# Hard graph attention with residual and layer norm: three steps of the item loop in another order on ScalarE and VectorE

## Chip, cores and metric

One core of a Trainium2 chip. The metric is the device time in microseconds (us) of the whole program, median of several runs.

## What is computed

```python
Q, K, V = (x @ W.T).reshape(n, 8, 32).transpose(1, 0, 2)      # n = 4096, one W each
attn = einsum('hqd,hkd->hqk', Q, K) * 32 ** -0.5 + (Q @ we.T + be)
attn = attn + where(adj > 0, 0.0, -inf)
attn = softmax(attn, axis=-1)
hard = (attn == max(attn, axis=-1, keepdims=True)) / 8
out  = einsum('hqk,hkd->hqd', hard, V).transpose(1, 0, 2).reshape(n, 256)
y    = layernorm(x + out)                                     # over 256 columns
```

Only the best permitted key of each query and head counts. The adjacency matrix is thin, and thinner for later rows.

## The kernel before

**Tiling.** 4096 rows are 32 tiles of 128 rows, a tile is 4 groups of 32 queries. The keys that at least one query of a group reaches are listed, and an item is up to 372 of them (3 chunks of 124). The loop scores 201 items here. For each item the kernel finds the key numbers, gathers rows of keys and values from `kv_table` in HBM, scores them, finds the minimum of the negated scores for each row and half of the heads, marks the winners, and adds their values to `o_all`.

**The loop.** After a first part (projections, table, the lists of 4 tiles) every engine runs the same loop. A turn is four bodies, b = 0 to 3, one item further each. Flags, planned by SyncE and read from memory, say whether a turn also has: the *front end* of a tile (`fe_on`: adjacency cast to bf16 in four quarters, packed into words), its *finish* (`fin_on`: ranks and lists), and *rows due* (`te_on`: transpose, residual and layer norm of a finished tile). A turn with none of them is called plain here. Engines meet only through semaphores, and each takes its instructions in the order written.

**Body b on each engine, in order** (item numbers relative to the turn):

- TensorE: `planes_of(b+4)` (L1207), `scores(b+1)` (L1222, L1227), `words` of a cast quarter (L1162) if there is one, `values(b-1)` (L1257), `hards_across(b)` (L1237), `keys_across(b+2)` (L1245), and for b = 1 `rows_back` (L1267). `words` and `values` wait for the merge of the item before.
- ScalarE: `masks(b+2)` (L656), `hard_rows(b)` (L652, waits for `hards_across(b)`), `owners(b+5)` (L624: the owner matrix `reached`, which `planes_of` of that item needs), `keys(b+2)` (L662, both halves), then the extras (b = 1: cast 1; b = 2: cast 3 at L605 and behind it `row_std` at L673), `hards(b+1)` (L667, waits for the minimum), and for b = 0 and 1 casts 0 and 2.
- VectorE: `pick(b+4)` (L928, L934, L941, L943: key numbers and mask bits), the extras, `tops(b+1)` (L951 `best`, L955 `minus_top`, L958 `keep`), for b = 2 `norm_rows` (L992 `rstd`, L995 `y_out`, which waits for ScalarE's `std`), and `merge(b-1)` (L968, two instructions).
- GpSimd: a copy of the queries (L525) and `gather(b+3)` (L532: three indirect DMAs, one for a chunk), which waits for the picks of its item.

`owners(b+5)` waits for `planes_of(b+3)` (two buffers `reached`), a step that TensorE does before `scores(b)`.

Of the kernel before, what the change touches and what calls it, by code (L numbers as in the profile page):

```python
# [5 lines left out]
ALU = mybir.AluOpType  # L6
# [32 lines left out]
def hard_attention(nc, x, adj, wq, wk, wv, we, be, out):  # L39
# [24 lines left out]
    with ExitStack() as ctx:  # L64
# [192 lines left out]
        def for_loop(eng, r, k):  # L257
            def value(s, j=0):
                ahead = k + j - lag[s.name]
                return r["n"] if ahead == 0 else eng.snap(r["n"]) + ahead  # L260
            return value
# [80 lines left out]
        def tile_of(eng, r, k):  # L342
            return eng.snap(r[k]) & (2 * T - 1)
# [239 lines left out]
        def _(act):  # L583
# [70 lines left out]
            def masks(m, due):  # L654
                act.wait_ge(dve_bits, due(dve_bits))
                act.activation(masked[m % RING][0:USED], bits[m % RING][0:USED].rearrange("p c l k -> p c (l k)")  # L656
                               .unsqueeze(2).to_broadcast([USED, CHUNKS, HEADS4, GQ]), ACT.Relu, bias=one[0:USED],
                               scale=-1.0).then_inc(act_masked, 1)
# [23 lines left out]
            def turn():  # L682
                def cast_quarter(i):
                    with front_end(act, r):
                        cast(tile_of(act, r, "fe") * 16 + 16, tile_of(act, r, "fe") * QUARTERS, i)

                for b in range(RING):
                    masks(b + 2, for_loop(act, r, 2))
                    hard_rows(b, for_loop(act, r, 0))
                    owners(b + 5, for_loop(act, r, 5), f"ahead{b + 5}")  # L690
                    for h in range(HALVES):
                        keys(b + 2, for_loop(act, r, 2), h)
                    if b == 0:
                        with front_end_finish(act, r):
                            flags_back(tile_of(act, r, "fin") + 1)
                    if b == 1:
                        cast_quarter(1)
                    if b == 2:
                        cast_quarter(3)
                        with rows_due(act, r):  # L700
                            row_std(tile_of(act, r, "te_done"))
                    if b == 3:
                        take_plan()
                    hards(b + 1, for_loop(act, r, 1))
                    if b == 0:
                        cast_quarter(0)
                    if b == 1:
                        cast_quarter(2)
                    act.reg_add(r["n"], r["n"], 1)
# [13 lines left out]
        def _(dve):  # L723
# [224 lines left out]
            def tops(m, due, at, between=None):  # L948
                dve.wait_ge(pe_score[0], due(pe_score[0]))
                dve.wait_ge(pe_score[1], due(pe_score[1]))  # L950
                dve.tensor_reduce(best[:], ps_both[m % 2][:, :, 0:SLOTS], AX.X, ALU.min).then_inc(dve_best, 1)  # L951
                if between is not None:
                    between()
                capped = cap_of[:].rearrange("p g i -> p (g i)")[:, bass.ds(at, 1)]
                dve.scalar_tensor_tensor(out=minus_top[m % 2][:], in0=minus_top[(m + 1) % 2][:], scalar=capped,  # L955
                                         in1=best[:], op0=ALU.max, op1=ALU.min
                                         )._wait_ge(dve_best, due(dve_best)).then_inc(dve_minus, 1)
                dve.scalar_tensor_tensor(out=keep[m % RING][:], in0=minus_top[(m + 1) % 2][:], scalar=capped,  # L958
                                         in1=minus_top[m % 2][:], op0=ALU.max, op1=ALU.is_equal
                                         )._wait_ge(dve_minus, due(dve_minus)).then_inc(dve_keep, 1)  # L960

            def merge(m, due, group):
                width = PARTS * HD
# [98 lines left out]
            def turn(begun=True):  # L1062
                def fin():
                    return tile_of(dve, r, "fin")

                def table():
                    return (dve.snap(r["fin"]) & (TABLES - 1)) * GPT

                for b in range(RING):
                    if b == 2:  # L1070
                        with front_end_finish(dve, r):
                            rank_steps(fin() + 1, fin() * FIN, table(), for_loop(dve, r, 4)(pe_planes))
                    pick(b + 4, for_loop(dve, r, 4), next_flags if b == 3 else None, "ahead8" if b == 0 else f"ahead{b + 4}")
                    if b == 1:
                        with front_end_finish(dve, r):
                            ranks(fin() + 1, fin() * FIN, None)
                            lists(fin() * FIN, table(), fin() * GPT)
                        with rows_due(dve, r):
                            odd = bits_of(dve, r["te_done"], 1)
                            with dve.If_lt(odd, 1):  # L1080
                                turn_rows(0, for_loop(dve, r, -2)(dve_merge))
                            with dve.If_ne(odd, 0):
                                turn_rows(GPT, for_loop(dve, r, -2)(dve_merge))
                    if b == 2:
                        with rows_due(dve, r):
                            norm_stats(tile_of(dve, r, "te_done"))
                    tops(b + 1, for_loop(dve, r, 1), listed(f"listed{b + 1}"),
                         (first_places, lambda: step_plan(dve, r), ended_places, next_places)[b])
                    if b == 0:
                        with front_end_finish(dve, r):  # L1090
                            dve.wait_ge(pe_pv, for_loop(dve, r, -1)(pe_pv))
                            word_steps(fin() + 1, fin() * FIN, table())
                    if b == 3:
                        with front_end(dve, r):
                            dve.wait_ge(pe_pv, for_loop(dve, r, -1)(pe_pv))
                            words(tile_of(dve, r, "fe") * QUARTERS, tile_of(dve, r, "fe") * FIN)
                        dve.reg_add(r["fe"], r["fe"], r["fe_on"])
                        dve.reg_mov(r["fe_on"], r["fe_next"])
                    if b == 2:
                        with rows_due(dve, r):  # L1100
                            norm_rows(tile_of(dve, r, "te_done"))
                    if b > 0 or begun:
                        merge(b - 1, for_loop(dve, r, -1),
                              dve.snap(r[f"running{b - 1}" if b else "running_last"], min_val=0, max_val=(2 * GPT - 1) * HALVES * PARTS * HD))
                    dve.reg_add(r["n"], r["n"], 1)

            turn(False)
# [294 lines left out]
```

## Time and profile before

| | us |
|---|---|
| median of 3 runs | 1316.35 |
| lowest, highest | 1309.31, 1316.83 |
| the profiled execution, its own time | 1317.37 |
| its span, first to last instruction | 1315.6 |
| busy in the span: TensorE matmul, VectorE, ScalarE, GpSimd | 951.6, 929.0, 892.0, 632.8 |
| VectorE `best` L951, 201 instructions | 190.7 |
| first and last `best` start at | 180.9, 1279.8 |

The mean granted TensorE clock of the span is 0.918 of full speed. No engine is busy over 72% of the span. The item loop lies between 181 and 1280 us, so about 1099 us for 200 bodies.

### The profile page before, as it was taken

The page shows a single profiled execution, that of the slowest core. Times are in us where ns is not written, and L with a number is a line of the kernel's source. Part 1 is how long each engine was busy: PE and PEld are TensorE (multiplying, and loading weights), DVE is VectorE, ACT ScalarE, POOL GpSimd, SP SyncE. Part 2 cuts the span into 40 slices and gives each one's busy share as a digit, 9 for nine tenths or more (in the row PEclk, how much of TensorE's full clock was granted, in tenths as well). Part 3 has the DMA queues.
Part 4 walks back from the last instruction along what each step waited for, and adds up shares of the span by engine and source line. Part 5 has one row for each costly group of instructions (what it writes and reads, how often), then busy time and mean ns, then how long its engine had stood idle before and what let it go on. Part 6 is the DMA issues. An engine that isn't in the chain of part 4 may idle for free.

```text
span 1315.6 us, 51593 instructions
## 1 busy us (share of the span) xinstructions
PE 951.6 (72%) x14758; PEld 616.6 (47%) x14759; DVE 929.0 (71%) x2616; ACT 892.0 (68%) x1688; POOL 632.8 (48%) x820
## 2 busy tenths in 40 slices
PE   4787648777777778777787777777777777777771
PEld 2343325454544555455454545455445545455540
DVE  5444536777878777777787777777777777778880
ACT  1523347778777787777877877877777777766770
POOL 0000065675656566555565555554554455445650
PEclk9988877999999998989999899989998989989995
DMA  4634468677687787678777878778878787756770
GB/s 155 214 128 160 145 201 279 196 231 255 197 263 217 243 253 234 215 242 266 248 207 231 268 226 262 252 230 272 257 235 258 248 251 254 254 180 194 212 213 4
DMA packets 89522, 291.06 MB, mean 221 GB/s; under 512 B 16984, under 2 KB 30040, under 8 KB 89496
## 3 DMA queue, kind: packets, MB, share of 16 engines
q0 software_dynamic: 48720, 199.60, 49.5%
q1 hardware_dynamic: 40776, 91.15, 20.4%
q8 instruction: 12, 0.20, 0.1%
q14 instruction: 14, 0.11, 0.0%
HBM read 275.98 MB, written 14.71 MB: 221 GB/s over the span
## 4 chain that ended last, share of the span: by engine, by line
DVE 26%; PE 25%; issue 20%; ACT 15%; DVEq 7%; DMA 3%; ACTq 2%; SPq 1%; POOL 1%; POOLq 0%
DVE best L951 6%; ACT joined L605 5%; PE ps_both L1222 4%; ACT k_t L662 4%; PE ps_both L1154 4%; DVE picks L941 3%; PE ps_h L1237 3%; PE ps_o L1257 3%; DVE hit_vals L934 3%; PE ps_r L1267 3%; DVE hit L928 2%; PE ps_both L1227 2%; ACT hard L667 2%; PE ps_both L1144 2%; DVE o_all L968 2%
## 5 line engine op out<-in xcount | busy, mean ns | idle before, releaser
L532 POOL DMA_INDIRECT kv<-kv_table,picks x309 | 294.9, 954 | 231.3 <-DVE picks L941 127.6
L532 POOL DMA_INDIRECT early<-kv_table,picks x300 | 286.2, 954 | 246.0 <-DVE picks L941 131.6
L652 ACT ACTIVATE hard_t<-ps_h 128x768 bf16<-128x768 bf16 x200 | 162.0, 810 | 233.1 <-PE ps_h L1237 227.4
L667 ACT ACTIVATE hard<-ps_both,minus_top 128x384 bf16<-128x384 f32 x402 | 214.1, 594 | 32.9 <-DVE minus_top L955 30.3
L1222 PE MATMUL ps_both<-k_t,q_now 32*32 32x384 f32 x3216 | 192.6, 534 | 32.1 <-ACT k_t L662 29.0
L951 DVE TENSOR_REDUCE best<-ps_both 128x2 f32<-128x768 f32 x201 | 190.7, 949 | 28.0 <-PE ps_both L1227 17.8
L1207 PE MATMUL ps_x<-pay,reached 128*128 x1224 | 120.2, 233 | 99.6 <-ACT reached L624 93.3
L662 ACT COPY k_t<-ps_both 128x384 f32<-128x384 f32 x404 | 171.6, 479 | 14.4 <-PE ps_both L1245 14.3
L968 DVE SCALAR_TENSOR_TENSOR o_all<-o_all,keep,ps_o 128x96 f32 x400 | 107.7, 311 | 61.8 <-issue 26.5
L1207 PEld LDWEIGHTS ps_x<-pay,reached 128*128 128x128 bf16 x1224 | 83.7, 102 | 137.5 <-ACT reached L624 128.0
L605 ACT ACTIVATE joined<-adj_in,minus_half 128x1024 bf16<-128x1024 int32 x128 | 147.9, 1164 | 0.0
L1227 PEld LDWEIGHTS ps_both<-mask_of,masked 128*128 128x128 bf16 x1206 | 72.9, 102 | 140.9 <-issue 140.9
L525 POOL COPY q_now<-q_t 128x64 f32 x202 | 50.4, 249 | 167.4 <-issue 164.3
L656 ACT ACTIVATE masked<-bits,one 124x384 bf16<-124x384 uint32 x202 | 127.6, 631 | 1.4 <-issue 1.4
L624 ACT ACTIVATE reached<-iota_h,edge_of 128x384 bf16<-128x384 f16 x205 | 124.1, 605 | 1.3 <-DVE pay L906 0.8
L1227 PE MATMUL ps_both<-mask_of,masked 128*128 128x128 bf16 x1206 | 109.4, 231 | 0.0
L1237 PE MATMUL ps_h<-ident_b,hard 128*128 128x128 bf16 x1200 | 107.6, 229 | 0.0
L941 DVE TENSOR_REDUCE picks<-hit_vals 128x9 uint32<-128x288 f32 x204 | 92.7, 455 | 15.1 <-DVE hit_vals L934 9.8
L934 DVE TENSOR_TENSOR hit_vals<-ps_x,hit 128x288 f32<-128x288 f32 x204 | 93.3, 458 | 7.0
L1245 PE MATMUL ps_both<-ident_f,kv 128*128 128x128 f32 x612 | 87.6, 281 | 12.0 <-DMA kv<-kv_table,picks 12.0
L1245 PE MATMUL ps_both<-ident_f,early 128*128 128x128 f32 x600 | 90.5, 291 | 1.6 <-DMA early<-kv_table,picks 1.6
L928 DVE SCALAR_TENSOR_TENSOR hit<-ps_x,slot_of,slot 128x96 f32<-128x96 f32 x204 | 64.0, 314 | 31.5 <-issue 16.1
(145 smaller groups left out, 1309.5 us busy)
## 6 DMA issues: line engine op xcount, KB each, us to landing
adj_in<-in_adj SPq DMA_DIRECT2D x128, 512.0 KB, 5.7
kv_table<-early SPq DMA_DIRECT2D x32, 320.0 KB, 2.4
kv<-kv_table,picks POOLq DMA_INDIRECT x309
early<-kv_table,picks POOLq DMA_INDIRECT x300
early<-in_x SPq DMA_DIRECT2D x8, 512.0 KB, 6.8
x_row<-in_x SPq DMA_DIRECT2D x32, 128.0 KB
out<-y_out SPq DMA_DIRECT2D x32, 128.0 KB
plan<-places_of SPq DMA_DIRECT2D x212, 0.0 KB
```

Of the source, the lines that this page charges most:

```text
L532: pool.indirect_dma_start(kv[m % KVS][:, c, :], None, kv_table, bass.IndirectOffsetOnAxis(ap=picks[m % RING][:, c, 2:3], axis=0)).then_inc ...
L605: act.activation(joined[:, i * QW:(i + 1) * QW], adj_in[:, i * QW:(i + 1) * QW], ACT.Sign, bias=minus_half[:]).then_inc(act_cast, 1)
L652: act.activation(hard_t[m % 2][:], hard_rows_t, ACT.Copy, bias=1.0).then_inc(act_hard_t, 1)
L662: act.copy(k_t[m % 2][:, h, :], ps_s[m % 2][h][:, 0:SLOTS]).then_inc(act_kt[h], 1)
L667: done = act.activation(hard[m % 2][:, h, :], ps_s[m % 2][h][:, 0:SLOTS], ACT.Sign, bias=minus_top[m % 2][:, h:h + 1], scale=-1.0)
L951: dve.tensor_reduce(best[:], ps_both[m % 2][:, :, 0:SLOTS], AX.X, ALU.min).then_inc(dve_best, 1)
L968: done = dve.scalar_tensor_tensor(out=o_run, in0=o_run, scalar=keep[m % RING][:, h:h + 1], in1=ps_o[:, h * width:(h + 1) * width], op0=ALU ...
L1207: mm = pe.matmul(ps_x[:, c * P:(c + 1) * P], reached[m % 2][:, c * P:(c + 1) * P], pay[:].rearrange("p g i v -> p (g i v)") [:, bass.ds(va ...
L1222: pe.matmul(ps_s[m % 2][h][to:to + GQ, 0:SLOTS], q_now[m % RING][head:head + HD, h, :], k_t[m % 2][head:head + HD, h, :], start=True, stop ...
L1227: mm = pe.matmul(bank[:, c * P:(c + 1) * P], masked[m % RING][:, c, :, :].rearrange("p h q -> p (h q)"), mask_of[:], start=False, stop=(c ...
L1237: mm = pe.transpose(hard_rows_t[:, at:at + P], hard[m % 2][:, h, c * P:(c + 1) * P], ident_b[:])
L1245: mm = pe.transpose(ps_s[m % 2][h][:, c * P:(c + 1) * P], kv[m % KVS][:, c, h * P:(h + 1) * P], ident_f[:])
```

## The change

On ScalarE `owners(b+5)` goes to the head of the body, ahead of `masks` and `hard_rows`; in body 2 `row_std` goes ahead of cast 3. On VectorE `keep` is computed from `best` itself (is_le in place of is_equal against `minus_top`), ahead of `minus_top`, which then carries no wait of its own; in body 2 `merge` goes ahead of `norm_rows`. No instruction is added or taken out, and nothing else changes.

```diff
                 for b in range(RING):
+                    owners(b + 5, for_loop(act, r, 5), f"ahead{b + 5}")
                     masks(b + 2, for_loop(act, r, 2))
                     hard_rows(b, for_loop(act, r, 0))
-                    owners(b + 5, for_loop(act, r, 5), f"ahead{b + 5}")
...
                     if b == 2:
-                        cast_quarter(3)
                         with rows_due(act, r):
                             row_std(tile_of(act, r, "te_done"))
+                        cast_quarter(3)
...
+                dve.scalar_tensor_tensor(out=keep[m % RING][:], in0=minus_top[(m + 1) % 2][:], scalar=capped,
+                                         in1=best[:], op0=ALU.max, op1=ALU.is_le
+                                         )._wait_ge(dve_best, due(dve_best)).then_inc(dve_keep, 1)
                 dve.scalar_tensor_tensor(out=minus_top[m % 2][:], in0=minus_top[(m + 1) % 2][:], scalar=capped,
-                                         in1=best[:], op0=ALU.max, op1=ALU.min
-                                         )._wait_ge(dve_best, due(dve_best)).then_inc(dve_minus, 1)
-                dve.scalar_tensor_tensor(out=keep[m % RING][:], in0=minus_top[(m + 1) % 2][:], scalar=capped,
-                                         in1=minus_top[m % 2][:], op0=ALU.max, op1=ALU.is_equal
-                                         )._wait_ge(dve_minus, due(dve_minus)).then_inc(dve_keep, 1)
+                                         in1=best[:], op0=ALU.max, op1=ALU.min).then_inc(dve_minus, 1)
...
+                    if b > 0 or begun:
+                        merge(b - 1, for_loop(dve, r, -1), ...)
                     if b == 2:
                         with rows_due(dve, r):
                             norm_rows(tile_of(dve, r, "te_done"))
-                    if b > 0 or begun:
-                        merge(b - 1, for_loop(dve, r, -1), ...)
```

## Rows read from the trace of the kernel before

**Rows 1.** The page, part 4: the chain that ended last, by engine.

```profile
DVE 26%; PE 25%; issue 20%; ACT 15%; DVEq 7%; DMA 3%; ACTq 2%; SPq 1%; POOL 1%; POOLq 0%
```

**Rows 2.** Timeline, one plain body: start us, us, engine, line, what, [idle before].

```profile
286.54 0.81 ACT L652 ACTIVATE hard_t<-ps_h 128x768 bf16<-128x768 bf16 x1 [0.86 <-PE ps_h L1237]
...
287.25 0.60 ACT L624 ACTIVATE reached<-iota_h,edge_of 128x384 bf16<-128x384 f16 x1
...
287.75 0.85 ACT L662 COPY k_t<-ps_both 128x384 f32<-128x384 f32 x2
...
287.90 0.56 PE L1207 MATMUL ps_x<-pay,reached 128*128 x6 [0.74 <-ACT reached L624]
...
288.74 0.88 PE L1222 MATMUL ps_both<-k_t,q_now 32*32 32x384 f32 x16 [0.28 <-ACT k_t L662]
...
290.91 0.81 ACT L652 ACTIVATE hard_t<-ps_h 128x768 bf16<-128x768 bf16 x1 [0.86 <-PE ps_h L1237]
```

**Rows 3.** Line 951 (`best`) in 299 to 878 us and 878 to 1203 us: how many bodies.

```profile
L951 DVE TENSOR_REDUCE best<-ps_both x109: 919/951/959, 298.9 to 878.0; 128x2 f32<-128x768 f32 x109
...
L951 DVE TENSOR_REDUCE best<-ps_both x53: 918/951/958, 878.0 to 1202.7; 128x2 f32<-128x768 f32 x53
```

**Rows 4.** Waits of VectorE, 299 to 878 us: total us, times, longest.

```profile
DVE rstd L992 <- ACT std L673: 35.9, 14, 3.2
```

**Rows 5.** Waits of VectorE, 878 to 1203 us.

```profile
DVE pay L906 <- PE ps_x L1207: 13.0, 13, 2.0
...
DVE rstd L992 <- ACT std L673: 6.7, 11, 0.8
```

**Rows 6.** Timeline, body 2 of a turn with front end and rows due.

```profile
606.25 0.18 DVE L988 BATCH_NORM_AGGREGATE mean_var<-stats 128x2 f32<-128x6 f32 x1
...
607.55 0.81 ACT L652 ACTIVATE hard_t<-ps_h 128x768 bf16<-128x768 bf16 x1 [0.92 <-PE ps_h L1237]
...
609.49 1.17 ACT L605 ACTIVATE joined<-adj_in,minus_half 128x1024 bf16<-128x1024 int32 x1
...
610.54 0.30 ACT L673 ACTIVATE std<-mean_var,eps 128x1 f32<-128x1 f32 x1
...
610.95 0.16 DVE L992 RECIPROCAL rstd<-std 128x1 f32<-128x1 f32 x1 [3.06 <-ACT std L673]
...
611.58 0.54 DVE L968 SCALAR_TENSOR_TENSOR o_all<-o_all,keep,ps_o 128x96 f32 x2
```

**Rows 7.** The chain in order of time, `minus_top` to merge: start us, us.

```profile
627.10 0.27 DVE minus_top L955
627.40 0.08 DVE keep L958
...
627.74 0.08 DVE o_all L968
```

**Rows 8.** Timeline of VectorE, three instructions with no wait between them.

```profile
581.41 0.29 DVE L881 SCALAR_TENSOR_TENSOR rank<-ps_x,flag 128x128 f32<-128x128 f32 x1 [0.26 <-issue]
581.62 0.15 DVE L883 COPY ends<-ps_x 128x4 f32<-128x4 f32 x1
581.68 0.15 DVE L884 SCALAR_TENSOR_TENSOR count_f<-ps_x,flag 128x4 f32<-128x4 f32 x1
```

**Rows 9.** Timeline of GpSimd in a plain turn: the first gather of three bodies running.

```profile
351.87 0.97 POOL L532 DMA_INDIRECT early<-kv_table,picks  x1 [0.16 <-issue]
...
357.39 0.97 POOL L532 DMA_INDIRECT early<-kv_table,picks  x1 [0.81 <-issue]
...
361.27 0.97 POOL L532 DMA_INDIRECT early<-kv_table,picks  x1 [0.16 <-issue]
```

**Rows 10.** Waits of ScalarE over the span.

```profile
ACT hard L667 <- DVE minus_top L955: 30.3, 38, 2.8
```

**Rows 11.** Timeline near the loop's start: scores at half clock, and VectorE behind planes.

```profile
198.97 1.53 PE L1222 MATMUL ps_both<-k_t,q_now 32*32 32x384 f32 x16
199.00 0.32 DVE L928 SCALAR_TENSOR_TENSOR hit<-ps_x,slot_of,slot 128x96 f32<-128x96 f32 x1 [1.80 <-PE ps_x L1207]
```

More of the change, by code:

```diff
@@ L1098, in turn @@
                         dve.reg_mov(r["fe_on"], r["fe_next"])
+                    if b > 0 or begun:
+                        merge(b - 1, for_loop(dve, r, -1),
+                              dve.snap(r[f"running{b - 1}" if b else "running_last"], min_val=0, max_val=(2 * GPT - 1) * HALVES * PARTS * HD))
                     if b == 2:
@@ L1101, in turn @@
                             norm_rows(tile_of(dve, r, "te_done"))
-                    if b > 0 or begun:
-                        merge(b - 1, for_loop(dve, r, -1),
-                              dve.snap(r[f"running{b - 1}" if b else "running_last"], min_val=0, max_val=(2 * GPT - 1) * HALVES * PARTS * HD))
                     dve.reg_add(r["n"], r["n"], 1)
```

## Prediction

> **What bounds the kernel now.** I read the page's chain first [rows 1]: no engine holds it; VectorE and TensorE have a quarter each, ScalarE 15%, and a fifth is issue, time in which an engine works through its own registers and waits. So two circles compete, and I looked for each in the timeline.
>
> The first is TensorE and ScalarE. In a plain body [rows 2] ScalarE starts `hard_rows` at 286.54, `owners` at 287.25, `keys` at 287.75; TensorE's planes wait for `owners`, its scores for `keys`; `values` and `hards_across` follow, and the next `hard_rows` starts at 290.91, the moment these end. One round is 4.37 us, and ScalarE has idled 0.86 us in front of `hard_rows`.
>
> The second is VectorE. From 299 to 878 us there are 108 bodies in 579.1 us, 5.36 each [rows 3]. Its one long wait there is `rstd` behind ScalarE's `std`: 35.9 us in 14 turns [rows 4]. Without it a body would be 5.03, nearly solid work and issue. From 878 to 1203 us every turn has everything in it: 52 bodies, 6.24 each, with only 6.7 us behind `std`, and 13.0 us in 13 waits for planes in front of L906 [rows 5]. VectorE is the bound there.
>
> Rows 6 show the stall whole. `mean_var` is ready from 606.43. ScalarE does `hard_rows` at 607.55, then owners and keys, then cast 3 at 609.49, and only then `std` at 610.54. VectorE has idled 3.06 us when `rstd` starts at 610.95, and its merge, which TensorE's next words and values wait for, comes at 611.58.
>
> **The change part by part.**
>
> *Owners first.* `owners` lies between `hard_rows` and `keys` and takes 0.50 us of that circle (287.25 to 287.75) [rows 2]. In front, it lies in the 0.86 us in which ScalarE waits for `hards_across`, so it costs nothing there; with that cover gone it would cost the same 0.50 again, so it never loses. Its own wait, planes of two items before, is over by then: TensorE does these ahead of the scores whose minimum the `hards` just before it in ScalarE's queue waited for. The circle falls from 4.37 to 3.87 in a plain body. Planes are no longer late either, as `reached` is there first. The gain counts only where this circle is the bound.
>
> *`std` ahead of cast 3, merge ahead of `norm_rows`.* `hard_rows` to cast 3 is 1.94 us, of which owners is 0.50; so `std` would start at 607.55 + 1.44 = 608.99 in place of 610.54, and `rstd` could start 0.41 later, at 609.40 [rows 6]. VectorE meanwhile does its merge (0.54 and its issue) first and is ready for `rstd` at about 608.6. In the phase of rows 6, 0.8 of the 3.06 us would be left. But the circle has by then run two bodies with 0.50 less each, so I take it that only the register work of about 0.2 us is left. Behind `std` in ScalarE's queue are cast 3 and `hards(3)`; `hards(3)` waits for a later VectorE result than `mean_var` in any case, and cast 3 comes 0.3 us later than it could. The merge comes at about 608 in place of 611.58, so TensorE no longer waits for it. Cost of the two moves on VectorE: nothing, the same instructions.
>
> Gain: 35.9 - 14 x 0.2 = 33.1 us in 299 to 878, and 6.7 - 11 x 0.2 = 4.5 us in 878 to 1203 [rows 4, 5].
>
> *`keep` first.* Now `minus_top` starts at 627.10, `keep` at 627.40, merge at 627.74 [rows 7]: 0.64 us, with `keep` and merge each behind a semaphore of the instruction just ahead. After it `keep` starts where `minus_top` did, `minus_top` needs no wait, and merge's wait is over while `minus_top` runs. Three instructions with no wait between them start 0.21 and 0.06 apart though they take 0.29 and 0.15: each starts some 0.08 ahead of the last one's end [rows 8]. So `minus_top` starts about 0.14 to 0.25 after `keep`, and merge 0.38 to 0.52 after it in place of 0.64. The trace shows no such pair of 128x2 instructions, so the bounds are 0.26 (merge issue alone decides) and 0.12 (strict order, the wait gone), and 0 if merge's issue work cannot start earlier. I take 0.18, in between, since the nearest rows overlap.
>
> The Trainium skill (VectorE: DVE Perf Modes, The DRAIN you can't avoid) says that chaining ops without semaphores saves nothing, as the next op waits for the pipe to empty; by that rule the sum would have nothing for `keep`. Rows 8 speak against it here, with starts ahead of the previous end; the page's own later section on two instructions with no wait allows an earlier start.
>
> The price: `minus_top` ends 0.14 to 0.26 us later after `best`, and `hards`, the cast behind it, and `hards_across` with it. ScalarE waits for `minus_top` in 38 of 200 bodies today [rows 10]. Where VectorE is the bound this comes back as nothing, since `hards` has a body's time until `hards_across`.
>
> *Where VectorE's gain stops.* In a plain turn GpSimd's gathers start 5.52 apart once and 3.88 apart otherwise [rows 9]: 5.52 + 3 x 3.88 = 17.2 us for four bodies, 4.29 a body, whatever the others do. Plain turns (20 bodies, 12 of them before 299 us) can thus hardly go under that; without this floor both circles would allow about 3.9. In 878 to 1203 body 1 of each turn waits for planes behind `rows_back` [rows 5], so what VectorE saves in that body is lost: 13 bodies.
>
> **The sum.**
>
> - 181 to 299 us, 24 bodies: in the first 8 the first circle binds (VectorE waits 1.80 for planes [rows 11]): 8 x 0.50 = 4.0. 4 more at 0.18: 0.7. 12 plain at 4.37 - 4.29: 1.0. Together 5.7.
> - 299 to 878: 33.1 for `std`; `keep` in 100 of 108 bodies (8 are plain): 18.0. I take off 3 for gathers that come late behind the two plain turns, and 3 for bodies in which the later `minus_top` does hold ScalarE. Together 45.
> - Can the first circle follow? It takes at most 5.36 a body now and loses 0.50: 4.86 or less. VectorE would be at 5.03 - 0.18 = 4.85. It can, just.
> - 878 to 1203: 4.5 for `std`, 39 bodies x 0.18 = 7.0: 11.5.
> - 1203 to 1280, 16 bodies x 0.18: 2.9.
>
> In all 65 us. The profiled execution took 1317.37, 1.0 above the median of the runs, so the sum gives 1252 by it and 1251 by the median: I say **1252**.
>
> **The rivals.**
>
> *The order of `keep` gives nothing* (strict order, or merge's issue work decides). For it: register work lies between `keep` and merge. Against it: rows 8. It takes away 0.7 + 18.0 + 7.0 + 2.9 = 28.6 us: 1281.
>
> *The first circle becomes the bound.* Casts stand behind `hards`, `hards` waits for a later `minus_top`, and words, values and `hards_across` stand behind the casts. If the 0.50 of owners counts in only half of the 108 bodies, that stage gives 27 in place of 45, and the rest about 15: 42 us, 1275. For it: 4.86 against 4.85 is no margin. Against it: much of the 5.36 is TensorE's wait for the late merge, which goes.
>
> *The stall stays.* `std` waits for `mean_var`, now with cast 3 queued behind it, and `keep` gives nothing: only the first 8 bodies gain, about 1310, no change. Against it: `mean_var` was ready 1.1 us before `hard_rows` began [rows 6].
>
> *Slower: the TensorE clock.* At the lower level (1.2 of 2.4 GHz) scores take 1.53 us in place of 0.88 [rows 11, 2]; scaled to planes, hards and keys too I estimate 2 us more a body. Planes now come right behind `keys_across` and leave one longer gap ahead of scores. If that gap lowers the clock in many bodies, it eats the gain: it takes about 32 more slow bodies to reach no gain and 40 to be 1% slower. TensorE is as busy for each item as before in less time, which speaks against it: 1335.
>
> **How the numbers follow.** Forecast 60% (its own range 1238 to 1268: `keep` at 0.12 to 0.26 moves it by 10 us either way, the two allowances by 6), `keep` for nothing 16%, first circle 12%, stall stays 6%, clock 6%. The range 1235 to 1283 takes in the first three but for their tails. 1% is 13 us, about what a measurement of this kernel tells from no change: faster 0.89, same 0.06, slower 0.05.
>
> **What would show it.** Right: the wait of `rstd` falls from 43 us in all to under 10; `owners` fills the idle time ahead of `hard_rows`; in a plain body `hard_rows` to `keys` is 0.71; `keep` to `minus_top` starts 0.14 to 0.25 apart and merge under 0.45 after `keep`; VectorE's waits for planes and best stay small; in plain turns GpSimd has no wait. Wrong: `rstd` still waits over 1 us; `best` waits for scores in most bodies (first circle); `minus_top` to merge is unchanged; a mean clock well under 0.918.

## The result, and the profile after

| us | before | after |
|---|---|---|
| median (lowest to highest) | 1316.32 (1309.31 to 1316.83) | 1247.07 (1242.54 to 1252.62) |
| span of the profiled execution | 1315.6 | 1247.1 |
| mean granted TensorE clock | 0.918 | 0.944 |
| busy: TensorE matmul, VectorE, ScalarE | 951.6, 929.0, 892.0 | 921.7, 913.0, 896.0 |

The ratio is 0.9488, with a 95% interval of 0.9436 to 0.9539: 5.1% faster, 69 us. The forecast of 1252 was 5 us too high. Executions of one kernel fall into two states some per cent apart, and the ratios below are of runs in the faster one, so they can differ slightly from the quotient of the medians, which are of all runs.

The chain that ended last, by engine, of the kernel after (to compare with [rows 1]):

```profile
DVE 35%; PE 19%; issue 17%; ACT 8%; DVEq 8%; DMA 7%; SPq 2%; POOL 2%; ACTq 1%; POOLq 0%
```

ScalarE has gone from 15% of the chain to 8%, and VectorE from 26 to 35%: the circle over ScalarE gave way, VectorE holds the loop more than before.

The starts of `best`, line 951 of the kernel after, in the stages that answer to those of [rows 3]:

```profile
L951 DVE TENSOR_REDUCE best<-ps_both x109: 918/951/959, 289.2 to 826.1; 128x2 f32<-128x768 f32 x109
...
L951 DVE TENSOR_REDUCE best<-ps_both x53: 917/951/959, 826.1 to 1138.4; 128x2 f32<-128x768 f32 x53
```

The same 108 bodies take 536.9 us in place of 579.1, the next 52 take 312.3 in place of 324.7.

The body of a turn with rows due, kernel after (timeline: start us, us, engine, line, what, [idle before]), against [rows 6]:

```profile
845.49 0.81 ACT L652 ACTIVATE hard_t<-ps_h 128x768 bf16<-128x768 bf16 x1 [1.93 <-PE ps_h L1236]
846.18 0.18 DVE L987 BATCH_NORM_AGGREGATE mean_var<-stats 128x2 f32<-128x6 f32 x1
...
846.93 0.32 ACT L673 ACTIVATE std<-mean_var,eps 128x1 f32<-128x1 f32 x1
847.13 1.16 ACT L605 ACTIVATE joined<-adj_in,minus_half 128x1024 bf16<-128x1024 int32 x1
...
847.34 0.22 DVE L955 SCALAR_TENSOR_TENSOR keep<-minus_top,cap_of,best 128x2 f32<-128x2 f32 x1
847.48 0.21 DVE L958 SCALAR_TENSOR_TENSOR minus_top<-minus_top,cap_of,best 128x2 f32<-128x2 f32 x1
847.68 0.54 DVE L967 SCALAR_TENSOR_TENSOR o_all<-o_all,keep,ps_o 128x96 f32 x2
848.24 0.16 DVE L991 RECIPROCAL rstd<-std 128x1 f32<-128x1 f32 x1
```

`std` starts 1.44 us after `hard_rows`, as worked out; it is over at 847.25, before VectorE begins `keep`, `minus_top` and merge, and `rstd` starts at 848.24 with no wait at all. The lines also show the new form of `keep`: `minus_top` starts 0.14 after it, merge 0.34 after it and 0.20 after `minus_top`; in [rows 7] merge came 0.64 after the first of the two.

A plain stretch after, against [rows 2]:

```profile
339.17 0.63 ACT L624 ACTIVATE reached<-iota_h,edge_of 128x384 bf16<-128x384 f16 x1
...
340.66 0.81 ACT L652 ACTIVATE hard_t<-ps_h 128x768 bf16<-128x768 bf16 x1 [0.35 <-PE ps_h L1236]
...
341.37 0.86 ACT L662 COPY k_t<-ps_both 128x384 f32<-128x384 f32 x2
```

The owner matrix fills the idle time ahead of `hard_rows`, which is 0.35 in place of 0.86, and `hard_rows` to `keys` is 0.71 in place of 1.21.

Waits of VectorE over the second stage, kernel after (total us, times, longest), against [rows 4]:

```profile
DVE hit L928 <- PE ps_x L1206: 17.3, 21, 2.0
...
DVE rstd L991 <- ACT std L673: 5.2, 10, 0.6
```

The stall at `rstd` fell from 35.9 to 5.2 us. The first line was small before (4.4 us in 10 waits): VectorE now waits 17.3 us at the head of `pick` for planes that TensorE has not done yet.

### The profile page after: what moved, and what is told of

It is laid out like the page before. It is cut to its first block, busy times and chain, and to the rows that moved or that the text cites. A ratio compares the mean times of both kernels' runs of the same rounds, so it can differ in the third digit from the quotient of the medians.

```text
span 1247.1 us, 51443 instructions
## 1 busy us (share of the span) xinstructions
PE 921.7 (74%) x14758; PEld 603.2 (48%) x14759; DVE 913.0 (73%) x2616; ACT 896.0 (72%) x1688; POOL 634.0 (51%) x820
## 4 chain that ended last, share of the span: by engine, by line
DVE 35%; PE 19%; issue 17%; ACT 8%; DVEq 8%; DMA 7%; SPq 2%; POOL 2%; ACTq 1%; POOLq 0%
DVE best L951 8%; DVE picks L941 5%; DVE hit_vals L934 4%; PE ps_r L1266 4%; PE ps_both L1153 4%; DVE hit L928 3%; ACT joined L605 3%; DMA early<-kv_table,picks 3%; DMA kv<-kv_table,picks 2%; PE ps_both L1143 2%; DVE o_all L967 2%; ACT hard_t L652 2%; DVE o_t L973 2%; DMA be_sb<-in_L_gnn_be 1%; PE ps_x L1206 1%
## 5 line engine op out<-in xcount | busy, mean ns | idle before, releaser
L667 ACT ACTIVATE hard<-ps_both,minus_top 128x384 bf16<-128x384 f32 x402 | 212.7, 586 | 98.0 <-DVE minus_top L958 87.3
L1221 PE MATMUL ps_both<-k_t,q_now 32*32 32x384 f32 x3216 | 182.1, 508 | 57.5 <-ACT k_t L662 54.5
L662 ACT COPY k_t<-ps_both 128x384 f32<-128x384 f32 x404 | 174.3, 489 | 23.5 <-PE ps_both L1244 23.1
L1206 PE MATMUL ps_x<-pay,reached 128*128 x1224 | 114.9, 225 | 39.1 <-issue 31.8
L1226 PEld LDWEIGHTS ps_both<-mask_of,masked 128*128 128x128 bf16 x1206 | 69.6, 99 | 131.2 <-issue 131.2
L624 ACT ACTIVATE reached<-iota_h,edge_of 128x384 bf16<-128x384 f16 x205 | 127.6, 622 | 2.9 <-issue 1.6
L656 ACT ACTIVATE masked<-bits,one 124x384 bf16<-124x384 uint32 x202 | 125.1, 619 | 0.0
L1236 PE MATMUL ps_h<-ident_b,hard 128*128 128x128 bf16 x1200 | 102.7, 222 | 6.8 <-ACT hard L667 5.0
L1226 PE MATMUL ps_both<-mask_of,masked 128*128 128x128 bf16 x1206 | 104.6, 224 | 0.0
L1244 PE MATMUL ps_both<-ident_f,kv 128*128 128x128 f32 x612 | 88.9, 283 | 17.2 <-DMA kv<-kv_table,picks 16.5
L1244 PE MATMUL ps_both<-ident_f,early 128*128 128x128 f32 x600 | 85.0, 278 | 10.5 <-DMA early<-kv_table,picks 10.0
```

The lines of the kernel that those rows point to most:

```text
L662: act.copy(k_t[m % 2][:, h, :], ps_s[m % 2][h][:, 0:SLOTS]).then_inc(act_kt[h], 1)
L667: done = act.activation(hard[m % 2][:, h, :], ps_s[m % 2][h][:, 0:SLOTS], ACT.Sign, bias=minus_top[m % 2][:, h:h + 1], scale=-1.0)
L1206: mm = pe.matmul(ps_x[:, c * P:(c + 1) * P], reached[m % 2][:, c * P:(c + 1) * P], pay[:].rearrange("p g i v -> p (g i v)") [:, bass.ds(va ...
L1221: pe.matmul(ps_s[m % 2][h][to:to + GQ, 0:SLOTS], q_now[m % RING][head:head + HD, h, :], k_t[m % 2][head:head + HD, h, :], start=True, stop ...
L1226: mm = pe.matmul(bank[:, c * P:(c + 1) * P], masked[m % RING][:, c, :, :].rearrange("p h q -> p (h q)"), mask_of[:], start=False, stop=(c ...
L1244: mm = pe.transpose(ps_s[m % 2][h][:, c * P:(c + 1) * P], kv[m % KVS][:, c, h * P:(h + 1) * P], ident_f[:])
```

## Experiments: one part at a time

All four ran on one chip, on which the kernel before took 1314.26 us (7 runs, 1313.43 to 1318.38). Each has 4 runs, and none of the intervals below takes in 1. The waits and stages are read from one profiled execution of each.

**Owners first alone.**

```diff
                 for b in range(RING):
+                    owners(b + 5, for_loop(act, r, 5), f"ahead{b + 5}")
                     masks(b + 2, for_loop(act, r, 2))
                     hard_rows(b, for_loop(act, r, 0))
-                    owners(b + 5, for_loop(act, r, 5), f"ahead{b + 5}")
```

> The kernel before with owners moved to the head of the body, nothing else. Theory A (VectorE is the bound of the new kernel, but before, one round of two turns runs partly over TensorE and ScalarE): owners alone shortens that part by 0.50 us a body, so the wait of rstd (43 us in all) falls by more than half, since two to four bodies lie between words and std; about 1316 - 32 = 1284, with rstd waiting about 15 us and the merge gap (minus_top start to merge) unchanged at 0.64 or more. Theory B (each part pays by itself and they add up; owners only where the circle binds, in the first bodies and the plain ones): about 1316 - 10 = 1306.

Measured: 1301.32 us, ratio 0.9892 (0.9861 to 0.9924): 13 to 14 us, near theory B. The wait of `rstd` fell by half all the same, from 43.0 to 22.3 us over the span, but not all of that shortened the program: in the second stage the wait fell by 17.7 us and the stage by 11.4.

**`keep` first alone.**

In short form, each instruction as its output, operands and operations:

```diff
+                keep   <- (minus_top[m + 1], capped, best; max, is_le), waits for best
-                minus_top <- (minus_top[m + 1], capped, best; max, min), waits for best
+                minus_top <- (minus_top[m + 1], capped, best; max, min)
-                keep   <- (minus_top[m + 1], capped, minus_top[m]; max, is_equal), waits for minus_top
```

> The kernel before with keep computed from best and put ahead of minus_top, nothing else. Theory A: VectorE is shortened by 0.26 us a body, but where a round runs over TensorE and ScalarE too the time goes into a longer rstd wait; only 39 bodies of the full turns and about half of the others gain: 1316 - 25 = 1291, rstd waits over 50 us. Theory B: all of 160 to 200 bodies gain 0.26: 1316 - 45 = 1271.

Measured: 1298.70, ratio 0.9864 (0.9835 to 0.9894): 16 to 18 us, less than either theory. The wait of `rstd` rose from 43.0 to 50.3 us, as theory A had it, and that for planes at `hit` in the second stage from 4.4 to 16.3.

**`std` ahead of cast 3 and merge ahead of `norm_rows`, alone.**

```diff
                     if b == 2:
-                        cast_quarter(3)
                         with rows_due(act, r):
                             row_std(tile_of(act, r, "te_done"))
+                        cast_quarter(3)
...
+                    if b > 0 or begun:
+                        merge(b - 1, ...)
                     if b == 2:
                         with rows_due(dve, r):
                             norm_rows(tile_of(dve, r, "te_done"))
-                    if b > 0 or begun:
-                        merge(b - 1, ...)
```

> The kernel before with std ahead of cast 3 on ScalarE and merge ahead of norm_rows on VectorE. Theory A: std comes 1.05 us earlier and the merge no longer waits for it; the rstd wait of 43 us falls to about 15: 1316 - 28 = 1288. Theory B (std and merge are all of the 33 + 4.5 us): 1279.

Measured: 1291.53, ratio 0.9823 (0.9788 to 0.9857): 23 us. That is theory A: 14.5 us of waits for `std` stay.

**All but `keep`** (the first and the third diff together).

> The changed kernel with minus_top and keep as before, so owners, std and merge alone. Theory A: VectorE is the bound nearly everywhere, so each body is longer by the 0.21 to 0.27 us that the intervals between two best show: 1247 + 45 = 1292 at most, 1285 if some bodies are bound by TensorE or the gathers. Theory B (the forecast's 0.18 a body and a bound elsewhere): 1247 + 28 = 1275.

Measured: 1274.65, ratio 0.9695 (0.9662 to 0.9728). The changed kernel is at 0.9488, so `keep` on top of the others is worth 27 us, as theory B had it, and more than alone. The three parts alone give 13, 16 and 23 us, 52 in all; together they give 69.

**Where each part pays.** The starts of the 1st, 25th, 133rd, 185th and last `best` in each timeline cut the loop into stages:

| us | to 25th | to 133rd | to 185th | to last |
|---|---|---|---|---|
| before | 118.0 | 579.1 | 324.7 | 77.1 |
| owners | 112.7 | 567.7 | 324.6 | 76.9 |
| keep | 116.4 | 572.0 | 321.1 | 73.9 |
| std and merge | 118.1 | 560.3 | 317.5 | 76.4 |
| all but keep | 110.3 | 548.8 | 322.4 | 76.6 |
| after | 107.5 | 536.8 | 312.3 | 73.2 |

In the second stage owners give 11.4, std with merge 18.8, both together 30.3: they add. `keep` gives 7.1 alone and 12.0 on top. In the last stage, with little else in a turn, `keep` gives 3.2 and 3.4 us over 16 bodies, 0.20 and 0.21 each.

**Why `std` needs owners.** Waits of VectorE in the second stage, std with merge alone:

```profile
DVE rstd L992 <- ACT std L673: 14.1, 12, 1.9
```

All but `keep`, the same stage; there is no line for `rstd` any more:

```profile
DVE o_all L968 <- DVE keep L958: 12.5, 28, 0.5
...
DVE hit L928 <- PE ps_x L1207: 6.6, 6, 1.3
```

Moved alone, `std` still comes late enough to cost 14.1 us; with 0.50 us less ahead of it in each body it costs nothing. The wait of 35.9 falls by 21.8 and 35.9, the stage by 18.8 and 30.3.

**Why `keep` gives less in that stage than its 0.27 a body.** In a body of the kernel before that waits for nothing the steps stand as follows:

```profile
352.48 0.22 DVE L955 SCALAR_TENSOR_TENSOR minus_top<-minus_top,cap_of,best 128x2 f32<-128x2 f32 x1
352.74 0.22 DVE L958 SCALAR_TENSOR_TENSOR keep<-minus_top,cap_of 128x2 f32<-128x2 f32 x1
353.08 0.54 DVE L968 SCALAR_TENSOR_TENSOR o_all<-o_all,keep,ps_o 128x96 f32 x2
```

And after:

```profile
355.71 0.22 DVE L955 SCALAR_TENSOR_TENSOR keep<-minus_top,cap_of,best 128x2 f32<-128x2 f32 x1
355.85 0.22 DVE L958 SCALAR_TENSOR_TENSOR minus_top<-minus_top,cap_of,best 128x2 f32<-128x2 f32 x1
356.04 0.54 DVE L967 SCALAR_TENSOR_TENSOR o_all<-o_all,keep,ps_o 128x96 f32 x2
```

From the first of the two to merge it is 0.60 before and 0.33 after: 0.27 less. Over 108 bodies that is 29 us. Against all but `keep`, the wait for planes grew from 6.6 to 17.3 and that of `rstd` from nothing to 5.2, 15.9 together; 29 - 16 = 13, and 12.0 was measured. VectorE is early, and what is behind it on the other engines is not.

**Why the third stage gives back a part of owners.** There std with merge alone take 317.5, and with owners added 322.4: owners *cost* 4.9. Waits of VectorE in this stage, std with merge alone:

```profile
DVE pay L906 <- PE ps_x L1207: 11.3, 13, 2.1
```

all but `keep`:

```profile
DVE pay L906 <- PE ps_x L1207: 16.3, 13, 2.4
```

and after:

```profile
DVE pay L906 <- PE ps_x L1206: 20.4, 13, 2.7
```

The 5.0 between the first two is as much as the loss. (Alone, owners give 0.1 us in this stage: what `rstd` waits less, L906 waits more.) What is ahead of L906 is on the chain that ended last, in order of time, kernel after:

```profile
862.58 0.99 DVE o_t L973
863.62 2.47 PE ps_r L1266 x12
866.08 0.43 PE ps_x L1186 x2
866.51 0.65 PE ps_x L1206 x6
...
867.56 0.30 DVE pay L906
```

TensorE's transposes of the finished rows (L1266) take 2.47 us. The same step with std and merge alone, from its timeline:

```profile
896.32 0.98 DVE L974 STREAM_TRANSPOSE o_t<-o_all 128x768 f32<-128x768 f32 x1 [0.68 <-DVE n_items L896]
...
897.35 1.60 PE L1267 MATMUL ps_r<-ident,o_t 128*128 128x128 f32 x12 [2.28 <-DVE o_t L974]
...
899.92 0.29 DVE L906 CAST pay<-ps_x 128x128 f32 x1 [0.57 <-PE ps_x L1207]
```

Start of `o_t` to L906 is 4.98 us after and 3.60 here. The windows over that stretch of the kernel after (us, busy time of PE, PEld, DVE, ACT, POOL, then the granted clock, DMA share, GB/s):

```profile
860.00:862.00 2.00, 1.09 (x12) 0.85 (x12) 1.43 (x8) 1.75 (x5) 0.97 (x1) 1.00 0.77 274
862.00:863.60 1.60, 0.00 (x0) 0.00 (x0) 1.02 (x2) 1.07 (x2) 1.07 (x2) 1.00 0.53 134
863.60:866.10 2.50, 2.48 (x14) 2.48 (x15) 1.69 (x5) 1.24 (x3) 1.07 (x2) 0.61 0.89 287
```

TensorE has nothing to do from 861.09 to 863.62, since `o_t` isn't there, and then runs most of the transposes at the lower level, 1.2 GHz, so that the clock of the window is 0.61. The transposes take 23.3 us over the stage with std and merge alone, 26.3 with owners, 27.5 after, and TensorE's own wait for `o_t` is 17.7, 34.7 and 31.7.

The 13 turns of the stage one by one say more than these two. From the start of `o_t` to L906 it is 3.61 us where the mean granted clock of that stretch is 0.92 to 1.00, and 4.1 to 5.4 where it is 0.53 to 0.81; no turn lies between:

| kernel | turns with the lower clock, of 13 | us over 3.60 in all turns |
|---|---|---|
| before | 4 | 5.4 |
| owners | 8 | 8.8 |
| keep | 4 | 4.7 |
| std and merge | 3 | 3.7 |
| all but keep | 6 | 8.6 |
| after | 7 | 9.2 |

The 8.6 less 3.7 is the 4.9 that owners cost here, and each of the three kernels with owners first has more such turns than each of the three without. As to the pause ahead of the transposes: with owners it is over 2.0 us in all 13 turns, without it is under 1.0 us in 6 to 8 of them. Over the six kernels, none of the 22 turns with a pause under 1.0 us has the lower clock, and 32 of the 56 with a pause of 1.8 us or more have. But the length of the pause does not tell which: the run with std and merge alone has a pause of 2.28 us here and the full clock, and behind pauses of 2.5 us and more 13 of 29 turns have it too. So the loss lies in the turns with the lower clock, and with owners first, which makes TensorE early, there are more of them. That a pause brings the lower clock about is what the counts suggest; no run took away the pause alone, and what else decides stays open.

## Experiments on two other chips

Two more groups of runs were made on two other chips, and there the kernel before itself took 1772.19 us (19 runs, 1752 to 1791) and 1775.45 (25 runs, 1747 to 1786), at a mean clock of 0.76 to 0.78. Below, "the first chip" stands for the runs in which the kernel before took 1314 to 1316. Whether the difference is one of chips or of the time at which they were used, no run tells. What was asked was how the parts go together and what is left; the numbers expected were for a kernel before at 1315, so none of the expected times can be met here.

**The changed kernel again**, on the first of these two chips.

> The changed kernel again, as the reference for the others of this chip: 1247, within 0.5%.

Measured: 1790.33, ratio 1.0134 (1.0037 to 1.023). The change gains nothing there. By the interval it loses 0.4 to 2.3%, but its four runs, 1780 to 1793, lie within the spread of the kernel before, and two kernels below that differ from it little (`minus_top` first; one more copy) measured 1.00 in ten runs each. Waits of ScalarE, this run:

```profile
ACT hard_t L652 <- remote: 544.4, 122, 6.6
ACT hard_t L652 <- PE ps_h L1236: 120.8, 67, 6.7
```

and of the changed kernel on the first chip:

```profile
ACT hard L667 <- DVE minus_top L958: 87.3, 92, 3.1
ACT hard_t L652 <- PE ps_h L1236: 83.0, 115, 3.1
```

One body there:

```profile
304.82 0.82 PE L1236 MATMUL ps_h<-ident_b,hard 128*128 128x128 bf16 x6
...
306.71 1.00 PE L1206 MATMUL ps_x<-pay,reached 128*128 x6
307.54 0.81 ACT L652 ACTIVATE hard_t<-ps_h 128x768 bf16<-128x768 bf16 x1 [3.73 <-remote]
307.58 0.54 DVE L967 SCALAR_TENSOR_TENSOR o_all<-o_all,keep,ps_o 128x96 f32 x2 [1.00 <-remote]
...
308.25 0.86 ACT L662 COPY k_t<-ps_both 128x384 f32<-128x384 f32 x2
...
309.25 0.88 PE L1221 MATMUL ps_both<-k_t,q_now 32*32 32x384 f32 x16 [1.54 <-ACT k_t L662]
```

By its record `hards_across` (L1236) ends at 305.64; ScalarE, which by the program waits for nothing else, starts at 307.54, 1.90 later, and the profile names no instruction that released it ("remote"). This gap is over 1 us in 126 of the 200 bodies, up to 4.3; with the same kernel on the first chip it is in one. ScalarE and VectorE are as busy as ever (898.1 and 922.3 us). So TensorE's results come late, `hard_t` with them, `keys` behind it, and the scores behind those (256.8 us of waits in 113, against 54.5 in 87). That is the first circle as the bound in most bodies, and with VectorE at 3% of the chain that ended last the savings on VectorE have little to save.

What holds TensorE there is open. The granted clock is lower too: `hards_across` ran at the lower level in 94 of 200 bodies, this one among them, against 3 with the same kernel on the first chip. That lengthens its steps (0.82 us in place of 0.51), but it is not the gap, which is over 1 us in 42 of the 77 bodies at the full clock as well. The profile puts 31% of the chain down to another core or an unknown queue, and the records of this core say no more.

**Owners at the end of the body, all else as changed** (the first diff undone), on both chips.

> The changed kernel with owners back behind hard_rows. Theory A (without the 0.50 us a body the circle of TensorE and ScalarE, up to 5.36 us before, is the bound again wherever casts are): two turns with front end and rows due take about 40.5 in place of 38.9, plain bodies 4.37; 1247 + 25 = 1272, with std late again (rstd waits over 12 us). But in the full turns owners early costs something by now (TensorE idles longer ahead of rows_back, and its slow clock runs showed 2.5 us for rows_back in place of 1.6), so these should be no slower without it. Theory B (VectorE alone is the bound): under 1255.

> The changed kernel with the owner matrix back at the end of the ScalarE's part of a body (order of before), keep, std and merge as changed. Theory A (each body pays the owner matrix where it lies between cast and hard rows; removed alone it gave 13 to 14 us, and its worth grows when the VectorE side is shorter, since both lie on one circle): 1269 to 1275 us, ratio 0.964 to 0.969, the body pitch of the first stage (best to best) 0.15 to 0.25 us longer than in the changed kernel. Theory B (the parts do not add: the owner matrix is hidden once keep leads): under 1257 us, ratio under 0.955.

Measured: 1859.79 and 1868.58; the second has a ratio of 1.0596 (1.0415 to 1.0777). On the first of these chips its four runs took 1828 to 1874 us, beside 1780 to 1793 of the changed kernel, 2% or more above: here the place of the owner matrix, which lies on the circle over TensorE, is worth much. Waits of TensorE in the second of these runs:

```profile
PE ps_x L1206 <- ACT reached L624: 291.0, 130, 4.7
```

With owners first this wait is 1.8 us. Why `keep`, `std` and merge without owners should be 4 to 8% *slower* than the kernel before there stays open: no run on those chips has them one by one.

**`minus_top` first, `keep` from `best` behind it, no wait between.**

```diff
-                keep   <- (minus_top[m + 1], capped, best; max, is_le), waits for best
-                minus_top <- (minus_top[m + 1], capped, best; max, min)
+                minus_top <- (minus_top[m + 1], capped, best; max, min), waits for best
+                keep   <- (minus_top[m + 1], capped, best; max, is_le)
```

> The changed kernel, but minus_top first with the wait on best, and keep second, still computed from best and with no wait of its own. It separates the order from the wait taken away. Theory A (what pays is that the second instruction has no wait and starts 0.14 us after the first in place of 0.26 to 0.30): merge then waits for keep, which ends 0.14 later than in the changed kernel, and hards gets minus_top 0.14 earlier; half of the 0.26 us is kept: 1247 + 10 to 20 = 1262. Theory B (order is what pays, since keep's wait must be over before merge's register work): 1247 + 27 = 1274, as without the step.

> The changed kernel with one order turned back: minus_top first behind best, keep after it, both without a wait between them (in the kernel before: minus_top, then keep which waits for it). Theory A (the gain of this part comes half from the wait between two VectorE instructions that is gone and half from the order, keep being what the merge needs): 1255 to 1265 us, ratio 0.953 to 0.961; the merge follows keep by about 0.2 us. Theory B (the order alone counts, since the wait is hidden): about 1274 us as with the old form of keep, ratio 0.968 to 0.970. Theory C (the wait alone counts): 1247 us, ratio 0.947 to 0.951.

Measured: 1777.14, ratio 1.0031 (0.9976 to 1.0085), and 1770.41, ratio 0.9988 (0.9917 to 1.0059). The times don't tell the wait from the order, since VectorE holds nothing there. The rows do, in a body of the second run in which merge waits for nothing:

```profile
510.86 0.22 DVE L955 SCALAR_TENSOR_TENSOR minus_top<-minus_top,cap_of,best 128x2 f32<-128x2 f32 x1
510.99 0.21 DVE L958 SCALAR_TENSOR_TENSOR keep<-minus_top,cap_of,best 128x2 f32<-128x2 f32 x1
511.19 0.54 DVE L967 SCALAR_TENSOR_TENSOR o_all<-o_all,keep,ps_o 128x96 f32 x2
```

The two start 0.13 to 0.14 apart, and merge follows 0.33 behind the first, just as with `keep` first. 0.33 is the least distance in both kernels. So the order is worth nothing on VectorE, and the whole 0.27 comes with the wait that is gone. The rows above fit: in both forms merge starts 0.33 to 0.34 behind the last instruction that waited, which before is the second of the pair (352.74 to 353.08) and after is the first (355.71 to 356.04). In that time VectorE's queue works through the register steps of merge. In the chain of [rows 7] two of them stand at 627.53 and 627.63, behind `keep` at 627.40; after, in the body at 847 us, one stands at 847.47, ahead of `minus_top` at 847.48. Nor does merge need the `keep` beside it: in body b it is `merge(b-1)` behind `tops(b+1)`, and reads a `keep` two items older. Computing `keep` from `best` was needed, since that is what lets the wait go; putting it first was not. What this kernel would take on the first chip is open.

**`rows_back` later: TensorE transposes the finished rows in body 2, behind the planes, not in body 1.**

```diff
                     planes_of(b + 4, ...)
+                    if b == 2:
+                        with rows_due(pe, r):
+                            rows_back(tile_of(pe, r, "te_done"))
...
-                    if b == 1:
-                        with rows_due(pe, r):
-                            rows_back(tile_of(pe, r, "te_done"))
```

> The changed kernel with rows_back moved on TensorE from the end of body 1 to behind planes_of of body 2. Theory A: in the 13 to 14 full turns VectorE waits 1.6 us a turn for planes, which stand behind rows_back and the rank step, while TensorE has idled 2.5 us ahead of rows_back for the transpose; with planes and rank step put into that idle time the wait of L906 (23.7 us in all) and half of hit's wait (23.2) go: 1247 - 25 = 1222. Theory B: rows_back then holds up scores and so best, and what L906 gains best loses: 1240 to 1250.

> The changed kernel with one step moved: TensorE issues the transposes of the finished rows (rows_back, and the GpSimd steps tied to it by the queue stay where they are) behind the planes of body 2 of a turn, not behind those of body 1. Theory A (the time that is left in the turns that finish a part lies in TensorE waiting for VectorE's o_t: 31.7 us in 13 ahead of rows_back in 826 to 1138, then 2.5 us for the transposes at a lower granted clock in place of 1.6): the wait goes to under 5 us in all, the transposes cost 1.5 to 1.6 us, and the time is about 1222 us, ratio to the kernel before 0.925 to 0.935. Theory B (the loop in these turns is held by the circle of VectorE and ScalarE and the wait of TensorE is idle time of an engine that is not the bound): 1240 to 1250 us, ratio 0.943 to 0.95.

Measured: 1764.12, ratio 0.9974 (0.9922 to 1.0026), and 1759.25, ratio 0.9987 (0.9923 to 1.005). It is not faster than the kernel before there. Beside the changed kernel on the same chip it is 26 us less, 1.5%, with the reserve on those four runs made above. VectorE's wait at L906 over the span, changed kernel and then this one, both on that chip:

```profile
DVE pay L906 <- PE ps_x L1206: 20.1, 16, 2.3
```

```profile
DVE pay L906 <- PE ps_x L1206: 5.4, 5, 1.7
```

The wait goes as theory A had it, while that of `rstd` rises from 26.8 to 38.3 us. But the third stage is only 8.7 us shorter (428.4 for 437.1), the second is 34.2 shorter and the last 14.5 longer, where the step hardly occurs: on this chip the bodies scatter more than the effect. Nor does it test the pause: the changed kernel there has a pause of over 1.1 us ahead of the transposes in one of the 13 turns only. Whether it gives its 25 us on a chip like the first is open, and worth a run.

**One more copy on GpSimd in each body** (128x256 to a buffer that nobody reads).

```diff
+                pool.tensor_copy(waste[m % RING][:], q_t[:, 0, 0:256])
                 pool.tensor_copy(q_now..., q_t...)
```

> The changed kernel with one more GpSimd instruction in each body, a copy of 128x256 to an unused buffer ahead of the copy of q (its result is read by nobody). It asks whether GpSimd's gathers hold the loop in plain turns. Theory A (the gathers now are the floor of a plain turn: the forecast's floor was 17.2 us a plain turn, turns took 15.1 to 16.1): each of its about 0.2 to 0.5 us enters the time, 1247 + 20 to 50 us, ratio 0.965 to 0.985, and the keys_across of TensorE waits longer for the DMA. Theory B (GpSimd has slack in most bodies, and only gathers behind a plain turn come late): 1247 to 1254 us, ratio 0.947 to 0.953.

Measured: 1774.98, ratio 1.0021 (0.9948 to 1.0094). The copy is 0.40 us long, some 80 us in all, and is not to be seen in the time: GpSimd has slack, as theory B says, but in a loop of 7.8 us a body that is no test of a plain turn of 3.8. For that only the trace of the kernel after speaks (below).

## Why the prediction was right, point by point

*By stage.* Predicted 5.7, 45, 11.5, 2.9, together 65; measured in the profiled executions 10.5, 42.3, 12.4, 3.9, together 69. The first stage gave nearly twice its term: owners beside `std` 7.8 in place of 5.0, and `keep` 2.8 in place of 0.7.

*The stall.* Right in place and size: predicted 33.1 and 4.5 us; with owners, all 35.9 went in the second stage. The step "the circle has by then run two bodies with 0.50 less each" is borne out by the run with std and merge alone, which leaves 14.1 us, and the one with owners added, which leaves nothing. At the end 5.2 came back with the new `keep`, by which VectorE is early again; alone it raises that wait from 35.9 to 41.1. In the third stage std and merge alone gave 7.2 in place of 4.5.

*Owners.* In the first stage 5.3 alone, against 4.0 + 1.0 in the sum. But beside `std` they were worth 7.8 there, and in the third stage they cost 4.9, which the sum had not at all: "it never loses" was right for ScalarE and wrong for what TensorE does with the time.

*`keep`: a term mis-sized twice, in opposite directions.* Its local saving was taken as 0.18 in 0.12 to 0.26 and is 0.27, just past the upper bound, because merge follows 0.33 after `keep` where 0.38 was my shortest. What holds is the case of that upper bound, merge's issue alone. The reason given was partly wrong: I took merge to wait for the instruction just ahead, and it waits for a `keep` two items older; by the run with `minus_top` first the saving does not come from the order at all. And its cover was taken as nearly full (18.0 of 108 bodies, 6 taken off), while 16 of its 29 us went into waits for planes and `std`. By stage `keep` on top of the others gave 2.8, 12.0, 10.1 and 3.4, against 0.7, 18.0, 7.0 and 2.9 in the sum. The sum had 28.6 for `keep` over the loop, and the run without it says 27. That two errors cancel is luck. The rival by which `keep` gives nothing was put at 1281; the kernel without it measured 1274.65.

*The rule of the Trainium skill* (VectorE: DVE Perf Modes, The DRAIN you can't avoid) that chaining without semaphores saves nothing: here a pair with the wait starts 0.26 apart and without it 0.14, so the measurement decides against it, for instructions of 128x2. It agrees with what the same section says of a next instruction that is not held, which starts earlier.

*The first circle as the bound.* On the first chip partly true: it shows as the 17.3 us of waits for planes. The sign "waits for planes stay small" thus failed, though the forecast held. On the other chips the trace looks like that rival, with TensorE late for a reason that is open.

*The later `minus_top`.* ScalarE waits for it 87.3 us in 92 bodies, against 30.3 in 38 [rows 10]. That is not the price of `keep`: with owners alone it is already 91.2 in 89. ScalarE is earlier, and idle.

*The floor of the gathers: wrong.* [rows 9] gave 17.2 us a plain turn. Its 5.52 held waits of that turn and is no cost of a gather. The mistake could be seen beforehand: four bodies before took 16.3. After, they take 15.3. What is true is that GpSimd falls behind in a plain turn. Its gathers there, kernel after, and who waits for them:

```profile
346.60 0.97 POOL L532 DMA_INDIRECT early<-kv_table,picks  x1 [0.16 <-issue]
...
350.33 0.87 PE L1244 MATMUL ps_both<-ident_f,early 128*128 128x128 f32 x6 [1.65 <-DMA early<-kv_table,picks]
350.48 0.97 POOL L532 DMA_INDIRECT kv<-kv_table,picks  x1 [0.16 <-issue]
...
351.92 1.38 PE L1221 MATMUL ps_both<-k_t,q_now 32*32 32x384 f32 x16 [0.21 <-ACT k_t L662]
```

The gathers start 3.88 us apart and wait for nothing, against bodies of 3.5 to 4.2; the debt is paid once, behind the turn, as 1.65 us of TensorE and then 1.38 for the scores in place of 0.88. Over the 11 bodies from the one ahead of this turn to the second turn behind it, `keep` saved 1.2 us against the kernel without it, in place of 11 x 0.27 = 3.0. So the 3 us taken off for two such turns was about right (some 1.8 in this one), for half the reason given.

*The clock.* The rival (lower in many bodies, 1335) did not come; the mean rose to 0.944. But its mechanism, a pause ahead of a TensorE step and then a lower clock, is what the third stage shows in 7 of 13 turns, at `rows_back` and not at the scores.

## To carry to other kernels

When two circles are near each other, cost the parts together and by stage: a part's worth depends on which circle is ahead, and of what an engine saves locally count only what the others can follow. An engine that is made early may idle ahead of a late input, and on TensorE the next step was then slower in about half of the turns here; look for whoever waits behind that step. On VectorE, small instructions of one chain gain from operands that let them stand side by side without a wait: what is behind them in the queue, register steps too, then starts earlier. Before you credit an order, look which item's result the next instruction reads.

## What the runs showed that was not expected

- Two VectorE instructions of 128x2 with no wait between start 0.13 to 0.14 us apart, each 0.22 long by its record; with the second waiting for the first, 0.26.
- 12 transposes of 128x128 f32 took 1.60 us at the full clock, and up to 2.93 where it fell. It fell in none of 22 turns with a pause under 1.0 us ahead of them, and in 32 of 56 with one of 1.8 us or more.
- The kernel before took 1314 and 1316 us on two occasions and 1772 and 1775 on two other chips. With the changed kernel on one of these, ScalarE and VectorE were busy for the same time and TensorE's results came over 1 us late in 126 of 200 bodies. There the change was worth nothing: its gain of 5.1% is shown only where TensorE's results come as soon as its records end.
